# P times V of a batch in one PSUM bank, the maxima turned in the other bank, and two chunks' reciprocals on VectorE

## The reference

```python
def adaln(x, c):                       # per batch b, per channel
    scale = clip(silu(c) @ scale_w.T + scale_b + 1, 0.1, 10)
    shift = silu(c) @ shift_w.T + shift_b
    norm = maximum(norm(x, axis=-1) * C ** -0.5, 1e-6)
    return x / norm * norm_w * scale + shift

x = x + softmax(mask(q @ k.T * 8 ** -0.5)) @ v @ proj_w.T + proj_b   # q, k, v of adaln(x, c)
h1, h2 = split(adaln(x, c) @ w1.T + b1)
x = x + (silu(h1) * h2) @ w2.T + b2
```

## Time and profile before

| | us |
|---|---|
| Median of 3 runs | 184.35 |
| Lowest, highest | 181.88, 184.48 |
| The profiled execution | 180.74 |
| Its span | 178.8 |
| PE, DVE, ACT, POOL busy in it | 146.9, 141.4, 134.7, 83.1 |
| `neg_max` L1107, 128 times | 81.5, idle before it 9.2 |
| `p_exp` L959, 128 times | 69.8, idle before it 15.7 |

### The profile page before, as it was taken

The page is one execution under the profiler, slowest core; times in us unless marked ns, Lnnn a source line. Parts: engine busy times, 40 slices in busy tenths (PEclk is TensorE's granted clock), DMA queues, the critical chain, the costliest instruction groups (busy, mean ns, idle before and its releaser), DMA issues.

```text
span 178.8 us, 3725 instructions
## 1 busy us (share of the span) xinstructions
PE 146.9 (82%) x1312; PEld 75.7 (42%) x1312; DVE 141.4 (79%) x248; ACT 134.7 (75%) x245; POOL 83.1 (46%) x133
## 2 busy tenths in 40 slices
PE   7778776668898889879769879788889976998992
PEld 7564233413333333333233333332225854785870
DVE  8756895978999999977999977996253947987992
ACT  8469862195897888958879958899877799599550
POOL 8319508965923304734618733335200525544650
PEclk9879999999999999999999999999999999999999
DMA  4847461537403375422022122022140300010103
GB/s 111 253 161 208 137 168 42 149 84 205 127 15 108 108 210 149 150 89 92 2 89 70 32 95 83 6 90 91 43 126 8 109 12 0 2 59 0 59 4 117
DMA packets 17512, 16.38 MB, mean 92 GB/s; under 512 B 2846, under 2 KB 16598, under 8 KB 17494
## 3 DMA queue, kind: packets, MB, share of 16 engines
q1 hardware_dynamic: 16086, 15.21, 27.6%
q0 software_dynamic: 1408, 0.93, 2.0%
HBM read 4.34 MB, written 5.24 MB: 54 GB/s over the span
## 4 chain that ended last, share of the span: by engine, by line
DVE 35%; PE 29%; issue 15%; ACT 10%; POOL 8%; DMA 2%; DVEq 0%; POOLq 0%; ACTq 0%
DVE neg_max L1107 24%; ACT p_exp L959 5%; POOL gated_lo L509 5%; PE bank L679 5%; PE bank L609 5%; PE bank L661 2%; DMA q_stack<-max_rows 2%; PE bank L635 2%; PE bank L630 2%; PE bank L564 2%; PE bank L728 2%; PE bank L529 1%; PE bank L553 1%; DVE rest L1082 1%; DVE k_stack L1017 1%
## 5 line engine op out<-in xcount | busy, mean ns | idle before, releaser
L1107 DVE TENSOR_REDUCE neg_max<-bank 128x2 f32<-128x512 f32 x128 | 81.5, 686 | 9.2 <-PE bank L609 8.8
L959 ACT ACTIVATE p_exp<-bank 128x512 f32<-128x512 f32 x128 | 69.8, 603 | 15.7 <-PE bank L661 14.6
L679 PE MATMUL bank<-p_exp,v_all 128*9 128x256 f32 x512 | 39.5, 381 | 0.3
L609 PE MATMUL bank<-k_stack,q_stack 62*128 62x256 bf16 x256 | 25.2, 271 | 17.2 <-DVE neg_max L1107 14.0
L509 POOL TENSOR_TENSOR gated_lo<-rs,gated_hi 128x512 fp32r<-128x512 f32 x14 | 18.2, 1302 | 28.8 <-ACT gated_hi L981 27.6
L473 POOL DMA_DIRECT2D q_stack<-max_rows x32 | 17.7, 556 | 22.7 <-DVE max_rows L1116 22.7
L661 PE MATMUL bank<-q_stack,k_stack 64*128 64x256 bf16 x256 | 25.3, 270 | 3.6 <-ACT p_exp L959 3.0
L609 PEld LDWEIGHTS bank<-k_stack,q_stack 62*128 62x128 bf16 x256 | 8.9, 93 | 43.4 <-DVE neg_max L1107 38.7
L463 POOL CAST max_parts<-neg_max 128x16 bf16<-128x16 f32 x16 | 3.1, 195 | 29.5 <-DVE neg_max L1107 29.5
L661 PEld LDWEIGHTS bank<-q_stack,k_stack 64*128 64x128 bf16 x256 | 12.2, 94 | 10.3 <-ACT p_exp L959 4.8
L728 PE MATMUL bank<-h_hi,w_parts 128*128 128x512 f32 x32 | 13.0, 407 | 1.6 <-DVE rs L1233 1.4
(11 more groups left out here) (115 smaller groups left out, 217.5 us busy)
## 6 DMA issues: line engine op xcount, KB each, us to landing
o_rows<-o_sb SPq DMA_DIRECT2D x16, 256.0 KB, 2.1
q_stack<-parts SPq DMA_DIRECT2D x18, 128.0 KB
k_stack<-parts SPq DMA_DIRECT2D x18, 128.0 KB
o_num<-o_rows SPq DMA_DIRECT2D x8, 128.0 KB, 2.4
o_den<-o_rows SPq DMA_DIRECT2D x8, 128.0 KB, 3.2
out_t<-o_num SPq DMA_DIRECT2D x8, 128.0 KB, 2.0
back<-back_w SPq DMA_DIRECT2D x1, 832.0 KB, 8.2
x_sb<-x_t SPq DMA_DIRECT2D x3, 256.0 KB, 4.9
```

What stands on the lines that cost most here:

```text
L609: mm = nc.tensor.matmul(scores[r][:, t * N:(t + 1) * N], q_stack[rows, c % STACKS, g, at + t * 128:at + (t + 1) * 128], k_stack[rows, c % ...
L679: mm = nc.tensor.matmul(bank[32 * j:32 * j + VW, 6 + k % 2, (q % 2) * N:(q % 2 + 1) * N], v_all[:, b, t, 2 * g + j, :], p_exp[:, (2 * q + ...
L959: nc.scalar.activation(p_exp[:, u % 4, par, :, :], bank[:, RING + v % RING, :].rearrange("p (t q) -> p t q", t=KT), ACT.Exp, scale=D ** -0 ...
L1107: nc.vector.tensor_reduce(out=neg_max[:, k % 2, :, par, g], in_=bank[:, n % RING, :].rearrange("p (t k) -> p t k", t=KT), axis=AX.X, op=AL ...
```

## The change

- `p_times_v` puts all 16 heads of a batch in one bank, `6 + b % 2`. Heads 0 to 7 take rows 32j to 32j + 8, heads 8 to 15 rows 32j + 16 to 32j + 24. So that both sides can add into the same rows, a weight tile is 25 columns wide: 9 that count and 16 zeros on the other side. `v_all` grows from 9 to 25 columns a head, and POOL has one memset more, of 128 x 4096 zeros.
- A batch is drained once: 8 drains (6 on ACT, 2 on DVE) and 8 stores in place of 16 each. `o_rows` is half as large.
- The turns from `k` = 2 on leave the ring and go to the bank of the batch they belong to, `6 + k // 2 % 2`, which holds nothing else at that time. So do the mean squares of chunks 0 and 1.
- Chunks 2 and 3 have no `ln_sum` and `inverse_sum`. DVE's `over_sum` takes a RECIPROCAL of 128 x 512 before its product. For chunk 2 it stands at `p` = 64 (was 65), its projection at 66 (was 67), its mean square at 69 (was 70).
- The Ln and Exp of chunk 2's inverse root stand right behind the last exponential, ahead of the first sigmoid. The table loads behind pair 3 are gone.
- The flags are written over the mask's tile, and `back_w`'s projection rows are put in the new order of channels on the host.

The diff, cut to its core:

```diff
@@ -66 +69 @@
-    P_SECOND_PART = (7, 8, 9, 11, 12, 14, 14, 15, 17, 19, 22)
+    P_SECOND_PART = (7, 8, 8, 11, 12, 14, 14, 15, 17, 19, 22)
 RING = 3
+RING_TURNS = 2
...
+def turn_bank(k):
+
+    return 6 + k // 2 % 2
+
+
+def square_bank(c):
+
+    return 6 + (BC * (c + 1)) % 2
...
-            nc.gpsimd.memset(v_all[:, :, :, :, D:VW], 1.0).then_inc(s_const, 1)
+            heads = v_all.rearrange("p b t h w -> p (b t h) w")
+            nc.gpsimd.memset(heads[:, :, D:VW], 1.0).then_inc(s_const, 1)
+            nc.gpsimd.memset(heads[:, :, VW:V_WINDOW], 0.0).then_inc(s_const, 1)
...
             def turn_maxima(k):
-                turned = ring_bank(item("turn", k))
+                if k < RING_TURNS:
+                    turned, done = ring_bank(item("turn", k)), s_a
+                else:
+                    turned, done = bank[:, turn_bank(k), :], s_turn
+                    if k % 2 == 0 and k >= 4:
+                        pe.wait_ge(s_od, k // 2 - 1)
+                    if k % 2:
+                        pe.wait_ge(s_turned, k - RING_TURNS)
...
             def p_times_v(q, t):
-                b, g = divmod(2 * q, G)
-                k = q // 2
+                b, quad = divmod(q, 4)
+                side, half = divmod(quad, 2)
...
                 for j in range(4):
-                    mm = nc.tensor.matmul(bank[32 * j:32 * j + VW, 6 + k % 2, (q % 2) * N:(q % 2 + 1) * N],
-                                          v_all[:, b, t, 2 * g + j, :],
+                    first = (4 * quad + j) * V_WINDOW - side * V_AT
+                    mm = nc.tensor.matmul(bank[32 * j:32 * j + V_WINDOW, 6 + b % 2, half * N:(half + 1) * N],
+                                          v_all[:, b, t, :, :].rearrange("p h w -> p (h w)")[:, first:first + V_WINDOW],
...
-                if u % 4 == 2 and 6 <= u < UNITS - 2:
-                    drain_output(u // 4 - 1)
+                if u % G == LAG and G < u < G * (B - 1):
+                    drain_output(u // G - 1)
                 for c in range(NC - 1):
                     behind = u - BC * G * (c + 1)
-                    if behind == P_LN_SUM:
+                    if c < EARLY and behind == P_LN_SUM:
                         ln_sum(c)
-                    if behind == P_INVERSE_SUM:
+                    if c < EARLY and behind == P_INVERSE_SUM:
                         inverse_sum(c)
...
+
+            ln_norm_2(NC - 2)
+            inverse_norm_2(NC - 2)
...
-                if n == AT_INVERSE_SUM:
-                    nc.scalar.preload_act_table_set("natural_log_exp_and_others")
-                    ln_norm_2(NC - 2)
-                    ln_sum(NC - 1)
-                    inverse_norm_2(NC - 2)
-                    inverse_sum(NC - 1)
...
             def over_sum(c):
-                dve.wait_ge(s_rec, 2 * c + 2)
+                dve.wait_ge(s_or[c], 32 * BC)
+                nc.vector.reciprocal(o_den[:, c, :], o_den[:, c, :]).then_inc(s_late_rec, 1)
+                dve.wait_ge(s_late_rec, c - EARLY + 1)
                 nc.vector.tensor_tensor(o_num[:, c, :], o_num[:, c, :], o_den[:, c, :], ALU.mult).then_inc(s_on, 1)
```

More of the change, by code:

```diff
@@ L26 @@
 VW = D + 1
+V_AT = 16
+V_WINDOW = V_AT + VW
 EPS = 1e-6
@@ L105, in ring_items @@
             items += [("scores", p, 0), ("scores", p, 1)]
-        items += [("turn", k) for k in range(HALVES) if turn_position(k) == p]
+        items += [("turn", k) for k in range(RING_TURNS) if turn_position(k) == p]
         items += [("project", c) for c in range(NC - 1) if project_position(c) == p]
-        items += [("square", c) for c in range(NC - 1) if square_position(c) == p]
+        items += [("square", c) for c in range(EARLY, NC - 1) if square_position(c) == p]
     return items
@@ L141, in drained @@
 def drained(n):
-    return sum(not (what[0] == "square" and what[1] < EARLY) for what in ITEMS[:n + 1])
+    return n + 1
+def turn_bank(k):
+    return 6 + k // 2 % 2
+def square_bank(c):
+    return 6 + (BC * (c + 1)) % 2
 def build(nc, x_t, small, mask, front_w, back_w, out_t):
-    o_rows = nc.dram_tensor("o_rows", [B, H, 32, N], F32).ap()
+    o_rows = nc.dram_tensor("o_rows", [B, 2, 4, 32, N], F32).ap()
     ctx = ExitStack()
@@ L378, in _ @@
                     stacks_of(e, j)
-            for k in range(HALVES):
-                if k == 3:
+            for b in range(B):
+                if b == BC - 1:
                     stacks_of(NP - 1, 0)
-                store_outputs(k)
-                if k % 2:
-                    load_outputs(k // 2)
-                if k == 3:
+                store_outputs(b)
+                load_outputs(b)
+                if b == BC - 1:
                     stacks_of(NP - 1, 1)
@@ L460, in _ @@
                 if k >= 2:
-                    pool.wait_ge(s_a, item("turn", k - 2) + 1)
+                    pool.wait_ge(*((s_a, item("turn", k - 2) + 1) if k - 2 < RING_TURNS else
+                                   (s_turn, k - 2 - RING_TURNS + 1)))
                 neg = neg_max[:, k % 2, :, :, :]
@@ L466, in _ @@
                                         ALU.subtract).then_inc(s_mp, 1)
-                pool.wait_ge(s_ad, drained(item("turn", k)))
+                pool.wait_ge(*((s_ad, drained(item("turn", k))) if k < RING_TURNS else (s_turned, k - RING_TURNS + 1)))
                 c, at = divmod(k // 2, BC)
@@ L586, in ring_bank @@
                 if n >= RING:
-                    if ITEMS[n - RING][0] == "square" and ITEMS[n - RING][1] < EARLY:
-                        pe.wait_ge(s_inv2, 2 * ITEMS[n - RING][1] + 1)
-                    else:
-                        pe.wait_ge(s_ad, drained(n - RING))
+                    pe.wait_ge(s_ad, drained(n - RING))
                 return bank[:, n % RING, :]
@@ L622, in turn_maxima @@
                                              ident[:, :])
-                mm.then_inc(s_a, 1)
+                mm.then_inc(done, 1)
             def project(c):
@@ L632, in mean_square_2 @@
             def mean_square_2(c):
-                squares = ring_bank(item("square", c))
+                if c < EARLY:
+                    squares, done = bank[:, square_bank(c), :], s_squares
+                    pe.wait_ge(s_turned, 4 * (c + 1) + 4 - RING_TURNS + 1)
+                else:
+                    squares, done = ring_bank(item("square", c)), s_a
                 pe.wait_ge(s_sq2, c + 1)
-                nc.tensor.matmul(squares, mean_w[:, :], sq2[:, c % 2, :], start=True, stop=True).then_inc(s_a, 1)
+                nc.tensor.matmul(squares, mean_w[:, :], sq2[:, c % 2, :], start=True, stop=True).then_inc(done, 1)
             def zero_outputs():
@@ L925, in ln_norm_2 @@
                 if c < EARLY:
-                    n = item("square", c)
-                    act.wait_ge(s_a, n + 1)
-                    nc.scalar.activation(rs2[:, c, :], bank[:, n % RING, :], ACT.Ln, bias=words[:, 2:3]).then_inc(s_inv2, 1)
+                    act.wait_ge(s_squares, c + 1)
+                    nc.scalar.activation(rs2[:, c, :], bank[:, square_bank(c), :], ACT.Ln,
+                                         bias=words[:, 2:3]).then_inc(s_inv2, 1)
                     return
@@ L1263, in turned @@
         return np.ascontiguousarray(np.asarray(a).T)
+    by_output = [(m % 2) * C // 2 + (m // 2) * D + d for m in range(H) for d in range(D)]
     by_row = [(2 * g + r) * D + d for r in range(2) for d in range(D) for g in range(G)]
```

84 lines of the change are left out of this document (47 added, 37 removed).

## The result

The changed kernel took 192.17 us (median of four runs, 189.63 to 192.82), the kernel before 183.68 beside it: 1.053 times as long, with an interval of 1.046 to 1.060. Medians here are of all executions, ratios of the fast ones, within about 1.5% of the kernel's fastest. The forecast was 185.0 and no change by 2%. The profiled execution took 192.25 us, its span is 190.4; the one before took 180.74, which is near the fastest of its kernel, so the traces stand 11.5 us apart where the medians stand 8.5.

A forecast was written before the change was run, and what follows sets the result against it. VectorE's maxima were taken to set attention's pace. The terms -3.4 - 1.0 + 3.0 + 2.0 gave +0.6 us against the profiled 180.74; put on the median of 184.35, that made 185.0 us, range 179.5 to 188.5.

The forecast's parts named there:

- Part 1: Attention: turns leave the ring, so VectorE's 0.38 us gap goes behind nine turns; 3.4 us gained.
- Part 3: Start: GpSimd's new 3.6 us memset shuts out VectorE's `any_diag`, on the path to the first unit; 3.0 us lost.
- Part 4: End of attention and MLP: two VectorE reciprocals of 3.1 us each delay TensorE's next pair; 2.0 us lost.
- Part 2: First chunk normalisation: VectorE starts ahead of GpSimd's product, so GpSimd waits and the operation is not lengthened; 1.0 us gained.
- The case in which the gap stays: Rival, attention: VectorE's gap moves and does not go, part 1 gives nothing; +4.0 us, 188.3 us, chance 0.03.

The follow-up runs named there:

- e5: Changed kernel with late memset, denominators and inverse roots as before, GpSimd's weight split behind turn 9 waiting for the first normalising operation; 176.42 us, 0.967 times the kernel before.
- e10: Kernel before, with GpSimd's weight split behind turn 9 made to wait for the first normalising operation; 183.34 us beside 183.62.
- e6: e5 with chunk 2's inverse root at the last exponential, its normalising ahead of the first pair, chunk 3's reciprocal on VectorE in halves; 177.02 us, 0.968 times the kernel before.
- e2: Changed kernel with GpSimd's zero memset at its place but waiting for VectorE's third small operation; 190.16 us, 1.045 times the kernel before.
- e7: e1 plus 14 clock-keeping matmuls in TensorE's hole ahead of the last projection; 184.89 us, 1.014 times the kernel before.
- e9: e6 plus nine clock-keeping matmuls ahead of unit 7's query scores; 176.50 us, 0.969 times the kernel before.
- e1: Changed kernel with GpSimd's zero memset moved behind its first k_stack transfers; 186.22 us, 1.021 times the kernel before.
- e4: e1 with only chunk 2's denominators put back on ScalarE; 183.44 us, 0.998 times the kernel before.
- e11: e5 with chunk 2's inverse root moved from behind pair 3 to the last exponential; 177.66 us, 0.977 times the kernel before.
- e8: e1 with both late reciprocals left out, and with them part of the computation; 177.56 us, 0.973 times the kernel before.

## Why the prediction was wrong

Between the two traces the forecast was +0.6 us and the measured change +11.6. Part 1 held. Parts 3 and 4 had the right cause and too small a size, +3.0 for +4.8 and +2.0 for +7.0. Part 2 had the wrong sign: -1.0 became a loss. The most costly step is the end of part 4: it let TensorE go on at full clock behind each hole, which cost about 3.3 us, and gave the normalising operations 0.9 us where they took 2.40.

- **Part 1, the ring: right.** Forecast -3.4 us. The gap is gone behind turns 4 to 7 (period 5.21 to 5.23; 5.30 forecast), nothing was gained at turns 8 and 12, where the idle time grew from 1.17 to 1.64 as foreseen. With the collision out of both kernels (e5 at 76.2 against e10 at 79.5, see above), copies 2 to 15 show -3.3.
- **Part 2, one collision less: the mechanism failed.** It looked at the two starts alone and concluded that "GpSimd is the one to wait". VectorE was 0.31 us ahead of the product and was held all the same, for GpSimd's whole 1.28 us: 2.15 = 0.67 + 1.28 and 0.2. Seven traces show it. Where GpSimd had been 0.14 ahead it was 1.70. What the step left out is that GpSimd was not idle: a DMA issue ran until 92.71 and the product began at 92.73. Where GpSimd was idle, a lead of 0.09 us was enough for VectorE (e6). The DMA issue alone does not hold VectorE (0.67 us beside it in e5), so what decides is not settled. The change made this collision longer, by 0.45 us, with a hole of 2.1 us on TensorE, and half clock behind it in six traces of seven. Forecast -1.0; the step from copy 9 to 10 shows +0.86, in spite of part 1. With the operation by itself, copies 2 to 15 are 4.3 us shorter than before (e5), which is the forecast's 4.4 for parts 1 and 2; the changed kernel shows 1.7.
- **Part 3, the memset: right in mechanism, too small.** +3.0 forecast, +4.8 measured. The duration was right (3.70 us for 3.6). The step that failed is the choice of `any_diag` as the operation shut out. It was the addition, five operations ahead of it, which was taken to get in as before. In e2 it does, and the comparison of the mask at 5.66, two operations ahead of `any_diag`, is shut out; that costs 3.85.
- **Part 4, the reciprocal: its duration right, its cost too small.** 3.33 us measured for 3.1, with 0.20 for 8 columns and 1.74 for 256: 6.2 ns for each further column. Forecast +2.0, measured +7.0. The working gave 2.1 us late for the first pair; it was 3.5, with a projection of 2.04 us at half clock in place of 1.13. In e2, with the full clock there, the pair is 2.3 late, so this step was right but for the clock. Behind pair 3 it took 0.9 us for the normalising operations, which took 2.40, since with ScalarE's pause gone they stand beside GpSimd's products: +1.5. And it ended the account at TensorE's next pair, at full clock: another 2.1 us were lost behind it, which e7 gives back.
- **A rival's sum.** The case in which the gap stays was put at +4.0. It kept part 2's gain of 1.0, which rested on the gap; without it the sum is +5.0.
- **The rest**: +1.5 us between copies 0 and 1 is most likely not the change's, since the work there is the same. Ahead of unit 7's query scores TensorE has a hole of 2.60 us in every kernel but e9. The step from copy 0 to 1 took 9.9 us in four of these traces and 11.1 to 12.9 in eight, at half clock behind the hole or soon after, the kernel before with one line more (e10) among the eight. The kernel before, run beside e1 to e4, itself took 180.84 us at a mean clock of 0.990 and 185.67 at 0.954.

The Trainium skill, page "SBUF — State Buffer", section "Who interferes with whom", says that the second to issue blocks for the whole instruction. The pair at 149.31 agrees: VectorE was first and GpSimd waited. e2 agrees in so far as the blocked one waits for the whole memset (4.00 us). The addition at 4.45 was not first either, since GpSimd's select ran until 4.67, but it also waited for the memsets that began after it. The operation at 92.42 does not agree: it began ahead of the product and waited for it.

## What to carry to other kernels

Price a stall on the engine that feeds TensorE twice: by its length, and by the half clock that may follow the hole. Before an operation of VectorE or GpSimd is moved or added, look at what the other one runs at that time and just before: a lead of 0.31 us did not help where GpSimd was busy, and one of 0.09 did where it was idle. A wait that parts them, where the other has slack, can be worth more than the change. Put a slow operation where its engine waits for something else, in pieces if need be. Here the packed bank, a late memset and one such wait gave 3.3% on a kernel which the change as a whole made 5% slower.

## What the runs showed of the hardware

- VectorE's operation on two SBUF inputs and GpSimd's tensor_tensor exclude each other. With GpSimd idle before, the first went first (0.47 us, and the product 1.54 for 1.29). With GpSimd issuing a DMA until 0.02 us before its product, VectorE waited although 0.31 us ahead (2.15 us for 0.67). GpSimd's memset held VectorE's tensor_scalar for its whole 3.7 us, but not a scalar_tensor_tensor of 128x512 (0.68 us in the midst of it, e1).
- An operation of 8 columns can starve behind a row of GpSimd's operations: 5.05 us, where it took 0.25 in e1.
- The reciprocal costs 6.2 ns for each further column: 1.74 us for 256, 3.33 for 512. A product of GpSimd beside it did not lengthen it (e6: 1.74 us at 133.13 and at 143.22).
- In or shortly behind a hole of TensorE its clock often came down to half, and matmuls of 0.39 us took 0.63: with 4.1 us idle in four traces of four, with 2.26 in three of four, with 2.60 in eight of twelve, with 2.10 in six of seven, and with 1.66 us in e11 and 1.67 in e9, but not with 1.62 in the kernel before. e8 and e9 also show half clock from about 20 us on, where TensorE had no hole of 1 us. What decides it stays open.
